# Splitting the Wv products of a fused perceiver block by head

## The chip, the cores and the metric

One core of one Trainium2 chip runs the whole program. The metric is the device time of one execution in microseconds (us), as the median of several runs. PE is TensorE, DVE is VectorE, ACT is ScalarE and POOL is GpSimd.

## What is computed

Three layers are added to `x` (8 batches x 64 queries x 256) one after the other: cross attention to a context of 1601 rows per batch with 16 heads of 64, a linear self attention with 8 heads, and a mixture of 8 experts of which each token takes 2. The change touches the cross attention alone, and in it only the product with the value weights. Cut to that:

```
xn     = layernorm(layernorm(x)) * gamma + beta
scores = (xn @ w_q)_h @ (context @ w_k)_h^T / 8        # per batch and head h
attn   = softmax(scores)
out_h  = attn_h @ (context @ w_v)_h                     # 64 x 64 per batch and head
x      = x + tanh(gate) * (concat(out_h) @ w_out + b_out)
```

The kernel never builds `context @ w_v`. It computes `U_h = attn_h @ context` (64 queries x 256) and then `U_h @ w_v_h` (256 x 64), which is the same by associativity.

## The kernel before, in words

The queries of two heads of one batch (2 x 64) fill 128 columns, and four such pairs make a group of 512 columns: 16 groups (`NG`), two for each batch. Within a group the 1601 context rows are taken in 13 steps of 128 (`SJ`; the last has 65). The kernel is written slot by slot, one slot per context step, 208 slots in all; the steps of one group are spread over later slots, so that the engines overlap. Each engine runs its own list in program order and waits on counting semaphores. 52 slots are written out, then a loop runs 3 times over 52 slots, then comes a drain in which the last group ends while the first 128-token tiles of the following layers (`chain`) begin.

In a slot PE does `scores` (six products of 512 columns in fp32r into the bank pair `sps`) and `times_context` (twelve products of some 256 columns in fp32r into `scp`), in some slots also transposes, and in slot 8 of a group (`V_WV`) `times_wv`, for the group two before. DVE and ACT make the softmax in between: `running_max`, `minus_max`, `exps`, `low_part`.

At the end of a group DVE normalises `U` (`take_u`, L903), PE transposes it in fp32 into `wps` (L1207), ACT copies it to `ut_sb` (L667), and `times_wv` multiplies it: for each of the four head pairs `t` and each half `dt` of the 256 context features one fp32 product. Its stationary operand is `wv_sb` of two heads (128 columns), its moving operand is `ut_sb[:, t, dt, :]`, the 128 query columns of the same two heads. The result is a 128 x 128 block in PSUM of which only the two 64 x 64 blocks on the diagonal mean something (head 0 with head 0's queries, head 1 with head 1's). The fp32 product appears in the trace as two pairs of a weight load (LDWEIGHTS) and a MATMUL, so a visit to `times_wv` is 8 products and 16 such pairs, and there are 16 visits. Then, in slot 9 (`V_O`), DVE's `take_o` copies the two diagonal blocks of all four pairs into `oT` with two instructions of 64 partitions x 256 (L911 and L912), and bank 0 of `wps` is free for the next `transpose_max`. `head_rows` is `(slice(0, 64), slice(64, 128))`, `Q` is 64, `P` is 128, `GT` is 4, `DT` is 2.

Other products of this kernel that have a part in what follows: L1334 (fp32, 128 weight columns, 64 moving columns), L1284 (fp32, 128 weight columns, 256 moving columns), L1424 (an fp32 transpose with 8 weight columns and 128 moving columns), L1431 (fp32, on 8 of the 128 rows, 128 weight columns, 256 moving columns), and L1367 (fp32r, 512 moving columns).

Of the kernel before, what the change touches and what calls it, by code (L numbers as in the profile page):

```python
# [34 lines left out]
P = 128  # L35
B, Q, D = 8, 64, 256
# [4 lines left out]
DT = D // P  # L41
TPB = H * Q // P
GT = 4
# [64 lines left out]
def linear(i, f):  # L108

    if isinstance(i, int):  # L110
        return f(i)
    return i * (f(2) - f(1)) + f(1)


def build(nc, x, ctx_n, ctx_t, gamma, beta, w_q, w_kt, w_v, w_out, b_out, gate, Wq, Wk, Wv, Wo, bo,
          W_router, b_router, W1, b1, W2, b2, out):
    with ExitStack() as es:
        def sb(name, shape, dt=F32):
            return es.enter_context(nc.sbuf_tensor(name, shape, dt))

        def sem(name):
            return es.enter_context(nc.semaphore(name))
# [97 lines left out]
        ut_sb = sb("ut_sb", [P, GT, DT, P])  # L220
# [45 lines left out]
        wps = es.enter_context(nc.psum_tensor("wps", [P, 2, 512], F32))  # L266
# [50 lines left out]
        o_ok = sem("o_ok")  # L317
# [23 lines left out]
        head_rows = (slice(0, Q), slice(Q, P))  # L341
# [32 lines left out]
        def small_h(f):  # L374

            return slice((f % (FT // 2)) * P, (f % (FT // 2) + 1) * P)
# [10 lines left out]
        def hbank(f):  # L387
            return [trp[0], trp[1], up, wp][f % 4]
# [404 lines left out]
        def _(dve):  # L793
# [11 lines left out]
            for r in range(2):  # L805
# [14 lines left out]
                for m in range(MT):  # L820
                    ins = dve.tensor_scalar(xn[:, m, :], src[:, m, :], mv[:, m, 0:1], rstd[:, m:m + 1],
                                            ALU.subtract, ALU.mult)
# [14 lines left out]
            for t in range(TPB):  # L837
# [4 lines left out]
                if t < 4:  # L842
                    ts_ = slice(t * TPB // 4, (t + 1) * TPB // 4)
# [61 lines left out]
            def take_o(i, u, tok):  # L905

                half = u // SJ % GPB
                ts_ = slice(half * GT, (half + 1) * GT)
                v = wps[:, 0, :].rearrange("p (t q) -> p t q", t=GT)
                dve.wait_ge(wv_ok, linear(i, lambda q: q * (PASS // SJ) + u // SJ - 1))  # L910
                dve.tensor_copy(oT[0:Q, ts_, tok], v[0:Q, :, 0:Q])  # L911
                dve.tensor_copy(oT[Q:P, ts_, tok], v[Q:P, :, Q:P]).then_inc(o_ok, 1)  # L912

            def slot(i, u, k):
                if L_SUB <= k < NSLOT + L_SUB:
                    minus_max(i, u - L_SUB)
                if L_LO <= k < NSLOT + L_LO:
                    low_part(i, u - L_LO)
                if 1 <= k <= NSLOT:
                    running_max(i, u - 1)  # L920
                if u % SJ == V_MR and SJ <= k < NSLOT + SJ:
                    column_max(i, u)
                if u % SJ == V_U and k >= 2 * SJ:
                    take_u(i, u)
                if u % SJ == V_O and k >= 2 * SJ:
                    b = u // (2 * SJ) - 1
                    if isinstance(i, int):
                        take_o(i, u, slice((i * 2 + b) * Q, (i * 2 + b + 1) * Q))
                    else:
                        take_o(i, u, bass.ds(i * (2 * Q) + (b + 2) * Q, Q))  # L930
# [194 lines left out]
        def _(pe):  # L1125

            pe.wait_ge(ident_ok, 1)
            for m in range(MT):
                pe.wait_ge(xn_ok, m + 1)
                for dt in range(DT):  # L1130
                    ins = pe.transpose(trp[dt][:, m * P:(m + 1) * P], xn[:, m, dt * P:(dt + 1) * P], ident[:])
# [4 lines left out]
            for t in range(TPB):  # L1136
                if t >= GT:
                    pe.wait_ge(pro_ql, t - GT + 1)
                for dt in range(DT):
                    if t == 0:  # L1140
                        pe.wait_ge(pro_trc, dt + 1)
                    ins = pe.matmul(scp[:, t % GT, :], wq_sb[:, dt, t * P:(t + 1) * P], xnT[:, dt, :],
                                    start=dt == 0, stop=dt == DT - 1)
# [4 lines left out]
            for t in range(TPB):  # L1148
                for dt in range(DT):
# [5 lines left out]
                    for c, (w, v) in enumerate(((wkt_hi, qT_hi), (wkt_hi, qT_lo), (wkt_lo, qT_hi))):  # L1155
                        for par in range(2):
                            ins = pe.matmul(scp[:, 2 * dt + par, :], w[:, par, t, dt * P:(dt + 1) * P], v[:, t, :],
                                            start=c == 0, stop=c == 2)
# [52 lines left out]
            def times_wv(i, u):  # L1211
                half = u // SJ % GPB
                if isinstance(i, int) and u == 2 * SJ + V_WV:
                    pe.wait_ge(tw_in, 16 * NTW)
                pe.wait_ge(utc_ok, linear(i, lambda q: (q * (PASS // SJ) + u // SJ - 1) * 2))
                for t in range(GT):
                    h0 = (half * GT + t) * P
                    for dt in range(DT):
                        ins = pe.matmul(wps[:, 0, t * P:(t + 1) * P], wv_sb[:, dt, h0:h0 + P], ut_sb[:, t, dt, :],  # L1219
                                        start=dt == 0, stop=dt == DT - 1)  # L1220
                ins.then_inc(wv_ok, 1)

            def transpose_max(i, u):
# [18 lines left out]
            def slot(i, u, k):  # L1242
                if k < NSLOT:
                    scores(i, u)
                if u % SJ == V_MT and SJ <= k < NSLOT + SJ:
                    transpose_max(i, u)
                if u % SJ == V_MB and SJ <= k < NSLOT + SJ:
                    spread_max(i, u)
                if L_PV <= k < NSLOT + L_PV:
                    times_context(i, u - L_PV)  # L1250
                if u % SJ == V_UT and k >= 2 * SJ:
                    transpose_u(i, u)
                if u % SJ == V_WV and k >= 2 * SJ:
                    times_wv(i, u)
# [154 lines left out]
            for f in range(FT):  # L1409
                c, n = h_cols(1), 0  # L1410
                for dt in range(DT):
                    for w, v in ((w1_hi, lnT_hi), (w1_hi, lnT_lo), (w1_lo, lnT_hi)):
                        ins = pe.matmul(hbank(f // (FT // 2))[:, small_h(f)], w[:, 0, dt, f * P:(f + 1) * P],
                                        v[:, dt, c], start=n == 0, stop=n == 5)
# [8 lines left out]
            for m in range(MT):  # L1423
                ins = pe.transpose(hbank(3)[0:NE, m * P:(m + 1) * P], gw[:, m, :], ident[:])  # L1424
# [5 lines left out]
            for m in range(MT):  # L1430
                ins = pe.matmul(hbank(2 + m // 2)[:, m % 2 * D:(m % 2 + 1) * D], gwT[:, m * P:(m + 1) * P], b2_sb[:],  # L1431
                                start=True, stop=True)
# [15 lines left out]
            for m in range(MT):  # L1448
                pe.wait_ge(yc_ok, (NE - 1) * MT + m - (MT - 1))
                ms = slice(m * P, (m + 1) * P)  # L1450
                for f in range(FT):
                    if m == 0:
                        pe.wait_ge(hl_ok, NE * FT + f + 1)
                    pe.matmul(scp[:, m, :], h_hi[:, f, ms], w2_sp[:, 1, f, :], start=f == 0, stop=False)
                    ins = pe.matmul(scp[:, m, 0:D], h_lo[:, f, ms], w2_sp[:, 1, f, 0:D],
                                    start=False, stop=f == FT - 1)
# [54 lines left out]
```

## Time and profile before

| | |
|---|---|
| median of 3 runs | 1005.5 us (1004.74 to 1005.71) |
| the profiled execution's own time | 1003.76 us |
| its span, first to last instruction | 1002.0 us |
| mean granted TensorE clock | 0.993 |
| PE busy (matmul) / PE weight loads | 952.7 us / 824.8 us |
| DVE busy / ACT busy / POOL busy | 751.1 / 503.6 / 571.3 us |

A record of a MATMUL lasts longer than the distance to the next one, because matmuls are pipelined; what a product costs is therefore read from start to start. Rows of the timeline merge equal neighbours: start, length of the whole run, and how many. Times in the timeline count from the start of the span.

### The profile page before, as it was taken

Reading aid. Unit: us, or ns where it says so; the run is one execution under the profiler, and the core shown is the slowest. Engines: PE = TensorE matmul, PEld = TensorE weight load, DVE = VectorE, ACT = ScalarE, POOL = GpSimd, SP = SyncE. Lnnn points to the kernel's source line nnn. Section 1 sums busy time; section 2 is a strip of 40 time slices with the busy share of each in tenths; the row PEclk is TensorE's granted clock in tenths of the full one; section 3 lists DMA queues with packets and bytes.
Section 4 is the critical chain, followed back from the end, with each engine's and each line's share of the span. In section 5 each row is a group of like instructions: output and inputs, shape, how many; then the busy total and the mean of one; then the engine's idle time right before and its main releaser. Section 6 shows DMA issues by size and latency. Waiting matters only on the chain.

```text
span 1002.0 us, 17582 instructions
## 1 busy us (share of the span) xinstructions
PE 952.7 (95%) x5732; PEld 824.8 (82%) x5732; DVE 751.1 (75%) x1181; ACT 503.6 (50%) x853; POOL 571.3 (57%) x609
## 2 busy tenths in 40 slices
PE   5899999999999999999999999999998699999998
PEld 2567988998889888899888888888886588888887
DVE  7647777977978868787787887876776676888776
ACT  3336655656565655556556565664452342433432
POOL 5767668948957866894895786730000342454440
PEclk9999999999999999999999999999999889999999
DMA  5584112211211221121221121101004022222200
GB/s 163 189 288 119 51 38 56 67 38 52 69 41 57 64 53 42 57 62 37 56 72 36 55 65 51 43 14 63 1 1 168 1 84 85 84 85 84 84 1 22
DMA packets 76182, 67.55 MB, mean 67 GB/s; under 512 B 7984, under 2 KB 72768, under 8 KB 76096
## 3 DMA queue, kind: packets, MB, share of 16 engines
q1 hardware_dynamic: 76096, 66.41, 22.2%
q8 instruction: 52, 0.85, 0.4%
q14 instruction: 34, 0.28, 0.1%
HBM read 58.01 MB, written 8.39 MB: 66 GB/s over the span
## 4 chain that ended last, share of the span: by engine, by line
PE 81%; DVE 12%; issue 2%; ACT 2%; DMA 2%; POOL 0%; SPq 0%; DVEq 0%; POOLq 0%
PE sps L1178 27%; PE scp L1193 9%; PE scp L1195 9%; PE scp L1194 9%; PE scp L1381 5%; PE sps L1367 5%; PE wps L1367 4%; PE wps L1219 3%; PE scp L1382 2%; DVE u_sb L903 2%; DMA qk_scratch<-oT 1%; DVE st L868 1%; DVE pt_lo L893 1%; PE sps L1284 1%; PE sps L1304 1%
## 5 line engine op out<-in xcount | busy, mean ns | idle before, releaser
L1193 PE MATMUL scp<-cn,pt_hi 128*128 128x258 f32 (+1 forms) x832 | 239.8, 288 | 3.6 <-DVE pt_lo L893 2.8
L1195 PE MATMUL scp<-cn,pt_lo 128*128 128x258 f32 (+1 forms) x832 | 234.9, 282 | 0.0
L1194 PE MATMUL scp<-cn,pt_hi 128*128 128x256 f32 (+1 forms) x832 | 234.9, 282 | 0.0
L650 ACT ACTIVATE st<-sps 128x512 f32<-128x512 f32 (+1 forms) x208 | 123.6, 594 | 159.2 <-PE sps L1178 158.3
L893 DVE TENSOR_TENSOR pt_lo<-st,pt_hi 128x512 fp32r<-128x512 f32 (+1 forms) x208 | 192.7, 926 | 7.2 <-ACT pt_hi L659 7.2
L868 DVE TENSOR_TENSOR st<-st,mbc 128x512 f32<-128x512 f32 (+1 forms) x208 | 156.6, 753 | 44.6 <-ACT mbc L673 37.3
L1178 PE MATMUL sps<-qk_hi,ct_hi 128*128 128x512 f32 (+1 forms) x416 | 167.8, 403 | 12.9 <-ACT st L650 5.6
L656 ACT ACTIVATE st<-st 128x512 f32<-128x512 f32 (+1 forms) x208 | 130.3, 626 | 93.9 <-DVE st L868 93.3
L1193 PEld LDWEIGHTS scp<-cn,pt_hi 128*128 128x128 f32 (+1 forms) x832 | 156.9, 189 | 13.7 <-DVE pt_lo L893 5.7
L1178 PE MATMUL sps<-qk_hi,ct_lo 128*128 128x512 f32 (+1 forms) x416 | 164.3, 395 | 0.0
L1194 PEld LDWEIGHTS scp<-cn,pt_hi 128*128 128x128 f32 (+1 forms) x832 | 157.3, 189 | 7.5 <-issue 0.2
L1178 PE MATMUL sps<-qk_lo,ct_hi 128*128 128x512 f32 (+1 forms) x416 | 163.4, 393 | 0.0
L558 POOL TENSOR_TENSOR cn<-raw,zero 128x256 fp32r<-128x256 f32 (+1 forms) x104 | 81.7, 786 | 133.8 <-PE scp L1195 122.6
L1195 PEld LDWEIGHTS scp<-cn,pt_lo 128*128 128x128 f32 (+1 forms) x832 | 157.8, 190 | 0.0
L879 DVE TENSOR_TENSOR cmax<-cmax,sps 128x512 f32<-128x512 f32 x192 | 130.7, 681 | 34.1 <-ACT st L650 33.5
L659 ACT ACTIVATE pt_hi<-st 128x512 fp32r<-128x512 f32 (+1 forms) x208 | 131.5, 632 | 7.6
L560 POOL TENSOR_TENSOR cn<-raw,cn 128x256 fp32r<-128x256 f32 (+1 forms) x104 | 99.1, 953 | 8.2
L1178 PEld LDWEIGHTS sps<-qk_hi,ct_hi 128*128 128x128 f32 (+1 forms) x416 | 76.6, 184 | 31.3 <-issue 11.9
L560 POOL TENSOR_TENSOR ct_lo<-raw,ct_hi 128x256 fp32r<-128x256 f32 (+1 forms) x104 | 95.7, 920 | 8.2
L558 POOL TENSOR_TENSOR ct_hi<-raw,zero 128x256 fp32r<-128x256 f32 (+1 forms) x104 | 93.5, 899 | 9.6 <-DMA raw<-ctx_t 9.6
L1178 PEld LDWEIGHTS sps<-qk_hi,ct_lo 128*128 128x128 f32 (+1 forms) x416 | 76.4, 184 | 20.2
L1178 PEld LDWEIGHTS sps<-qk_lo,ct_hi 128*128 128x128 f32 (+1 forms) x416 | 76.7, 184 | 10.4
(210 smaller groups left out, 1523.1 us busy)
## 6 DMA issues: line engine op xcount, KB each, us to landing
w_raw<-W SPq DMA_DIRECT2D x16, 1024.0 KB, 7.4
raw<-ctx_t SPq DMA_DIRECT2D x96, 128.0 KB, 2.2
raw<-ctx_n SPq DMA_DIRECT2D x96, 128.0 KB, 2.0
raw<-qk_scratch SPq DMA_DIRECT2D x60, 128.0 KB, 2.1
qk_scratch<-oT SPq DMA_DIRECT2D x4, 1024.0 KB, 6.1
qk_scratch<-oT SPq DMA_DIRECT2D x4, 896.0 KB, 4.2
wq_sb<-w_q SPq DMA_DIRECT2D x1, 1024.0 KB, 4.9
wkt_sb<-w_kt SPq DMA_DIRECT2D x1, 1024.0 KB, 7.8
```

Source lines behind the costliest of these rows:

```text
L558: pool.tensor_tensor(hi, src, z.broadcast_to(tuple(src.shape)), ALU.add).then_inc(split_hi, 1)
L560: pool.tensor_tensor(lo, src, hi.bitcast(F32), ALU.subtract).then_inc(done, 1)
L650: act.activation(st[0:rows(j), par, j, :], sps[0:rows(j), u % 2, :], ACT.Copy).then_inc(out_ok, 1)
L656: act.activation(p, p, ACT.Exp).then_inc(exp_ok, 1)
L659: act.activation(pt_hi[0:rows(j), r, :], p, ACT.Copy).then_inc(hi_ok, 1)
L868: dve.tensor_tensor(p, p, mbc[0:rows(j), par, :], ALU.subtract).then_inc(sub_ok, 1)
L879: dve.tensor_tensor(m, m, src, ALU.max).then_inc(max_ok, 1)
L893: dve.tensor_tensor(pt_lo[0:rows(j), r, :], st[0:rows(j), par, j, :], pt_hi[0:rows(j), r, :].bitcast(F32), ALU.subtract).then_inc(lo_ok, 1)
L1178: ins = pe.matmul(sps[0:rows(j), u % 2, :], a[:, dt, cols], v[:, par, dt, :], start=c == 0, stop=c == 5)
L1193: pe.matmul(scp[:, t, 0:D + 2], hi, cn[0:rows(j), j, 0:D + 2], start=j == 0, stop=False)
L1194: pe.matmul(scp[:, t, 0:D], hi, cn[0:rows(j), j, D + 2:CNW], start=False, stop=False)
L1195: ins = pe.matmul(scp[:, t, 0:D + 2], lo, cn[0:rows(j), j, 0:D + 2], start=False, stop=j == SJ - 1)
```

## The change

`times_wv` issues two products where it had one: for each head of the pair one with that head's 64 weight columns and that head's 64 moving columns, into 64 of the output partitions (0 to 63 for the first head, 64 to 127 for the second) and 64 columns of the bank. A visit then has 16 products in place of 8, and the two heads alternate. The results of the four pairs lie side by side in 256 columns, and `take_o` copies them with one instruction of 128 partitions x 256. Semaphores, slots and all other work stay.

```
@@ take_o
-                v = wps[:, 0, :].rearrange("p (t q) -> p t q", t=GT)
                 dve.wait_ge(wv_ok, linear(i, lambda q: q * (PASS // SJ) + u // SJ - 1))
-                dve.tensor_copy(oT[0:Q, ts_, tok], v[0:Q, :, 0:Q])
-                dve.tensor_copy(oT[Q:P, ts_, tok], v[Q:P, :, Q:P]).then_inc(o_ok, 1)
+                dve.tensor_copy(oT[:, ts_, tok],
+                                wps[:, 0, 0:GT * Q].rearrange("p (t q) -> p t q", t=GT)).then_inc(o_ok, 1)
@@ times_wv
                     for dt in range(DT):
-                        ins = pe.matmul(wps[:, 0, t * P:(t + 1) * P], wv_sb[:, dt, h0:h0 + P], ut_sb[:, t, dt, :],
-                                        start=dt == 0, stop=dt == DT - 1)
+                        for hr in head_rows:
+                            ins = pe.matmul(wps[hr, 0, t * Q:(t + 1) * Q],
+                                            wv_sb[:, dt, h0 + hr.start:h0 + hr.stop], ut_sb[:, t, dt, hr],
+                                            start=dt == 0, stop=dt == DT - 1)
```

## Rows read from the trace of the kernel before

**Rows 1.** The page: busy us of PE, and granted clock in 40 slices.
```profile
PE 952.7 (95%) x5732; PEld 824.8 (82%) x5732; DVE 751.1 (75%) x1181; ACT 503.6 (50%) x853; POOL 571.3 (57%) x609
PEclk9999999999999999999999999999999889999999
```

**Rows 2.** The page: the chain that ended last, shares of the span by line.
```profile
PE sps L1178 27%; PE scp L1193 9%; PE scp L1195 9%; PE scp L1194 9%; PE scp L1381 5%; PE sps L1367 5%; PE wps L1367 4%; PE wps L1219 3%; PE scp L1382 2%; DVE u_sb L903 2%; DMA qk_scratch<-oT 1%; DVE st L868 1%; DVE pt_lo L893 1%; PE sps L1284 1%; PE sps L1304 1%
```

**Rows 3.** The chain in order of time, 255 to 310 us: start, us, what.
```profile
261.34 1.78 PE wps L1219 x16
263.13 1.40 PE sps L1178 x6
```

**Rows 4.** All instructions on the tile wps: durations in ns min/median/max.
```profile
L1219 PEld LDWEIGHTS wps<-ut_sb,wv_sb x256: 187/192/192, 137.6 to 772.1; 128*128 128x128 f32 x128
...
L911 DVE COPY oT<-wps x16: 408/417/417, 139.7 to 772.9; 64x256 f32 x12, 64x256 f32<-64x256 f32 x4
L912 DVE COPY oT<-wps x16: 427/429/430, 140.1 to 773.3; 64x256 f32 x12, 64x256 f32<-64x256 f32 x4
```

**Rows 5.** Timeline of PE around one visit: start us, us, line, operation, tiles.
```profile
261.18 1.95 PE L1219 MATMUL wps<-ut_sb,wv_sb 128*128 128x128 f32 x16
262.88 0.48 PE L1178 MATMUL sps<-qk_hi,ct_hi 128*128 128x512 f32 x1
263.20 0.39 PE L1178 MATMUL sps<-qk_lo,ct_hi 128*128 128x512 f32 x1
```

**Rows 6.** Timeline of PE, 16 pairs with 64 moving columns.
```profile
733.16 1.95 PE L1334 MATMUL sps<-ke,cbd 128*128 128x64 f32 x16
734.94 0.61 PE L1311 MATMUL sps<-ident,ke 128*128 128x128 f32 x4
```

**Rows 7.** Timeline of PE, 16 pairs with 256 moving columns.
```profile
690.21 3.61 PE L1284 MATMUL sps<-wout_sb,oT 128*128 128x256 f32 x16
693.66 0.60 PE L1229 MATMUL wps<-ident,cmax 128*128 128x128 f32 x4
```

**Rows 8.** Weight loads of 65 columns (L1178, last context step), ns min/median/max.
```profile
L1178 PEld LDWEIGHTS sps<-qk_hi,ct_hi x2: 134/134/135, 230.0 to 230.6; 128*65 128x65 f32 x2
```

**Rows 9.** Timeline of PE around the products on 8 rows.
```profile
841.08 0.40 PE L1367 MATMUL sps<-lnT_lo,w_hi 128*128 128x512 f32 x1
841.31 0.39 PE L1367 MATMUL sps<-lnT_hi,w_lo 128*128 128x512 f32 x1
841.63 1.99 PE L1431 MATMUL wps<-b_sb,gwT 8*128 8x256 f32 x8
843.55 0.50 PE L1367 MATMUL sps<-lnT_hi,w_hi 128*128 128x512 f32 x1
843.89 0.39 PE L1367 MATMUL sps<-lnT_lo,w_hi 128*128 128x512 f32 x1
```

**Rows 10.** Timeline of PE around the transposes with 8 weight columns.
```profile
839.59 0.28 PE L1382 MATMUL scp<-w_sp,h_lo 128*128 128x256 f32 x1
839.70 0.60 PE L1424 MATMUL wps<-ident,gw 128*8 128x128 f32 x4
```

**Rows 11.** Timeline of DVE after one visit.
```profile
221.92 0.42 DVE L911 COPY oT<-wps 64x256 f32 x1 [1.53 <-PE wps L1219]
222.34 0.43 DVE L912 COPY oT<-wps 64x256 f32 x1
...
224.13 0.69 DVE L879 TENSOR_TENSOR cmax<-cmax,sps 128x512 f32<-128x512 f32 x1
```

**Rows 12.** Timeline of PE, the scores that wait for that maximum.
```profile
227.27 0.40 PE L1178 MATMUL sps<-qk_hi,ct_hi 128*128 128x512 f32 x1
```

**Rows 13.** Timeline of all engines after the last visit.
```profile
773.32 0.43 DVE L912 COPY oT<-wps 64x256 f32<-64x256 f32 x1
773.63 0.66 PE L1317 MATMUL sps<-ident,qe 128*128 128x128 f32 x4 [0.69 <-ACT kn L715]
774.12 3.62 PE L1284 MATMUL scp<-wout_sb,oT 128*128 128x256 f32 x16
```

## The prediction

> **What bounds the kernel.** I read the page first. PE is busy for 952.7 of 1002 us and its clock is granted almost throughout [rows 1]; a busy PE is not yet PE at its peak, so the next view is the chain of waits. It is made of PE's lines, with the changed line L1219 holding 3% of the span and no DVE line above 2% [rows 2]. In order of time, the reader should see the visit to L1219 stand in that chain with its whole length, 1.78 us, and the scores of the next slot follow at once [rows 3]. So whatever a visit gains or loses on PE goes one to one into the time, 16 times. 1% of the span is about 35% of what all visits cost (16 x 1.78 = 28.5 us), and that is the frame: a visit that vanished would be worth 2.8%.
>
> **What a visit costs now.** From its first MATMUL to the first of the scores are 1.70 us, and the next one comes after 0.32 us where 0.23 is usual in that row's stream (841.08 to 841.31); 1.70 + 0.09 = 1.79 us for 16 pairs of weight load and MATMUL, 111 ns a pair [rows 5, 9]. Two things could set these 111 ns. L1334 has half the moving columns (64) and the same 128 weight columns, and its 16 pairs take 1.78 us, 111 ns a pair: fewer moving columns alone buy nothing [rows 6]. L1284 has 256 moving columns and takes 3.45 / 16 = 216 ns a pair, 0.84 ns per moving column [rows 7]; 128 columns would be 108 ns. So now both sides, 128 weight columns and 128 moving columns, stand at the same height. The change halves both.
>
> **The new products.** A visit has 32 pairs with 64 weight and 64 moving columns. No row has such a pair. From the moving side: 64 x 0.84 = 54 ns. From the weight side: a load of 65 columns lasts 134 ns where one of 128 lasts 192 (L1219) [rows 4, 8]; that is some 0.9 ns a column, so 64 fewer take about 55 ns off the 111 and leave 56 to 57. The slower side sets the pace: 57 ns, and 32 x 57 = 1.82 us. The bounds are 54 ns a pair from [rows 7], and 111 ns if a pair has a floor of its own that [rows 6] can't be told from; faster than 54 only if the two heads overlap (a rival below). I take 57, because in [rows 7] a pair's time follows its columns with hardly a constant. Against 1.79 us this is +0.03 to +0.04 us a visit: half as many useless multiplications, but twice as many pairs at half the length, and the balance is zero.
>
> **Entering and leaving a part of the array.** The old products use all rows and all columns, as do all products around them; the new ones write 64 of the 128 output partitions. The trace has a block that uses part of the array, L1431 on 8 of 128 rows. The MATMUL before it is followed after 0.32 us instead of 0.23 (+0.09); its 8 pairs with 256 moving columns take 1.92 us where 8 x 0.216 = 1.73 (+0.19); and the first fp32r product after it takes 0.34 instead of 0.23 (+0.11). Together 0.39 us for going in and out, in which no weight load hides behind the MATMUL before [rows 7, 9]. In going in, a load of 64 columns is 0.055 us shorter than one of 128, so I take 0.33 us a visit; bounds 0 and 0.39. The nearest row against it is L1424: 8 weight columns, and it follows after the usual 0.11 us [rows 10], but it is a transpose and writes from partition 0, so nothing forces it into a part of the array, while the second head's output at partition 64 does. The Trainium skill (TensorEngine Tiling (Array Packing), Key Properties) says that a change of the tiling mode, not merely of the tile, drains TensorE. By that the columns pay as the rows do in [rows 9], and alternating between the two halves within a visit pays nothing; without the rule the cost of part columns would be as open as its two bounds, and the sum by it is the same +0.33.
>
> **DVE.** Two copies of 0.42 and 0.43 us become one of 128 x 256, which by their durations takes 0.43 us: 0.42 us less a visit [rows 4, 11]. It is hidden: DVE had idled 1.53 us for the visit, and the next thing that PE wants from behind the copies, the maximum that ends at 224.82, is wanted by the scores at 227.27, 2.4 us later [rows 11, 12]. Behind the last visit the copies end at 773.75, and the product that reads them starts only at 774.12, when L1317 has left PE [rows 13]. So 0; if the cover were gone the saving would be 16 x 0.42 = 6.7 us. A longer visit delays DVE and the softmax behind it by 0.37 us, well inside the same 2.4.
>
> **Sum.** 0.04 + 0.33 = 0.37 us a visit, 16 x 0.37 = 5.9 us. The profiled execution would go from 1003.76 to 1009.7 us; the median of the runs is 1.7 us above it, so 1005.5 + 5.9 = 1011.4 us. The likeliest case's own range is 1008 to 1014. About 0.2% (2 us) is what a measurement of this kernel can tell from no change.
>
> **Rival 1, faster: the halves overlap.** The two heads use different columns of the array and alternate, so each pair could run beside its neighbour. Then 16 double pairs at 57 ns are 0.91 us, with the 0.33 us of going in and out 1.24 against 1.79: -0.55 us a visit, 996.7 us; without the switch cost -0.88 us, 991.4 us. It decides from where the 32 pairs take under 1.79 - 0.33 = 1.46 us, 46 ns a pair. For it speaks that they share no output and no weights; against it that all weight loads in the trace follow each other at one load's length, in [rows 6] even where the moving side is half idle, so that the load path, which stays full (32 x 64 columns), would hold 57 ns. The trace has no pair of neighbours on different columns. The Trainium skill (same page and section) states that different tiles can load weights and multiply in parallel, with up to twice the speed at 64 columns; that is this rival, its time would be the 996.7 us, and no row here shows it. Chance 0.22.
>
> **Rival 2, no change: no switch cost for columns.** As in [rows 10], the loads go on hiding. Then 0.04 x 16 = 0.6 us: 1006.1 us. Chance 0.15.
>
> **Rival 3, much slower: a pair has a floor, or its load isn't hidden.** At 111 ns a pair, 32 take 3.55 us: +1.76, with the switch +2.09 us a visit, 1039 us. At 80 ns, half way, 2.56 us: +1.10, 1023 us. For it: no pair in the rows is shorter than 108 to 111 ns whichever side is small. The Trainium skill (TensorE: Matmul & The Clock Gate, Part 3) says that a weight load overlaps a MATMUL in flight only when it goes to other rows of the array; then load and MATMUL would add to some 111 ns, the 1039 us. The trace does not agree for full columns: 16 loads and 16 MATMULs of 108 ns and more each fit in 1.79 us [rows 5]. Chance 0.18, two thirds of it near 1023.
>
> **Numbers.** My forecast, serial pairs at their columns' length plus the switch, has 0.45, since the balance of zero rests on two rows and the switch on one that measures rows and not columns. Faster 0.24 (rival 1, and a little of DVE's saving surfacing), same 0.13, slower 0.63. The range of 8 in 10 leaves out the fast end of rival 1 and the slow end of rival 3: 996 to 1026 us.
>
> **What would show it.** A visit, from its first MATMUL to the scores, of about 32 x 57 = 1.8 us plus delays at both ends, with the first weight load no longer beside the MATMUL before it: right. A distance of 57 ns between MATMULs shows the pace, 28 shows overlap, 111 the floor. One copy of 0.43 us on DVE with idle time before it, and no new wait of PE for DVE. The prediction is wrong if the visit is shorter than 1.7 us, if the switch is missing, or if PE's clock or a loop's start moves the time by more than the visits do.

## The result, and the profile after

The changed kernel takes 995.19 us (median; 994.19 to 996.96, 4 runs) where the one before takes 1005.37 us: ratio 0.9901, 95% interval 0.9884 to 0.9919. Measured a second time, 996.25 us against 1005.02, ratio 0.9912 (0.9895 to 0.9928). The two profiled executions are 8.1 us apart: 995.64 us against 1003.76. It is faster by about 0.9%, where 0.6% slower was forecast. The case that occurred is rival 1.

The page of the changed kernel, busy time and granted clock (against [rows 1]):

```profile
PE 945.0 (95%) x5988; PEld 814.4 (82%) x5988; DVE 747.2 (75%) x1165; ACT 503.2 (51%) x853; POOL 570.7 (57%) x609
PEclk9999999999999999999999999999999799999999
```

PE has 256 MATMUL records more and is busy 7.7 us less. The clock is nearly as before, 0.991 on average against 0.993. In the chain in order of time (start, us, what) a visit still stands with its whole length, now 1.08 us where [rows 3] has 1.78:

```profile
259.40 1.08 PE wps L1219 x32
260.48 1.59 PE sps L1177 x6
```

The timeline of PE around one visit of the changed kernel, against [rows 5]:

```profile
218.26 0.28 PE L1194 MATMUL scp<-cn,pt_lo 128*128 128x258 f32 x1
218.47 1.15 PE L1219 MATMUL wps<-ut_sb,wv_sb 128*64 128x64 f32 x32
219.55 0.50 PE L1177 MATMUL sps<-qk_hi,ct_hi 128*128 128x512 f32 x1
219.90 0.39 PE L1177 MATMUL sps<-qk_lo,ct_hi 128*128 128x512 f32 x1
```

All 32 pairs of weight load and MATMUL fit in 219.55 - 218.47 = 1.08 us. Before them there are now 0.21 us to the last MATMUL of L1194 where 0.12 is usual (+0.09), and behind them the second product of the scores comes after 0.35 us where 0.23 is usual (+0.11). A visit costs 0.09 + 1.08 + 0.11 = 1.28 us. Before it cost 1.79. The weight loads of the same stretch show the way in and out: the first of the visit and the first of the scores start with their own MATMUL, not 0.11 us ahead of it.

```profile
218.47 1.01 PEld L1219 LDWEIGHTS wps<-ut_sb,wv_sb 128*64 128x64 f32 x32
219.55 0.19 PEld L1177 LDWEIGHTS sps<-qk_hi,ct_hi 128*128 128x128 f32 x1
```

How the 32 pairs lie can be read by counting the MATMULs of L1219 in ever longer windows from the visit's start. The columns are window, its length, PE busy with the count in brackets, granted clock, DMA share and GB/s:

```profile
218.46:218.50 0.04, 0.03 (x2) 1.00 0.76 256
218.46:218.57 0.11, 0.10 (x2) 1.00 0.53 177
218.46:218.60 0.14, 0.13 (x4) 1.00 0.53 176
218.46:218.63 0.17, 0.16 (x4) 1.00 0.47 157
218.46:218.66 0.20, 0.19 (x6) 1.00 0.43 144
```

They start two at a time, one of each head, and the next two follow after some 58 ns. That is the 57 ns I had expected of one pair, with two pairs in it. Only the first step is longer, since its weight load is not hidden. Sixteen steps of 58 ns are 0.93 us, so 0.15 of the 1.08 us belong to going in and out, as do the 0.09 and 0.11 beside the block: 0.35 us in all.

The period of two groups, from a visit to the second one after it, shows what it is worth. Before, from 261.18 [rows 5] to

```profile
343.39 1.95 PE L1219 MATMUL wps<-ut_sb,wv_sb 128*128 128x128 f32 x16
```

are 82.21 us. In the changed kernel

```profile
259.32 1.15 PE L1219 MATMUL wps<-ut_sb,wv_sb 128*64 128x64 f32 x32
...
340.43 1.15 PE L1219 MATMUL wps<-ut_sb,wv_sb 128*64 128x64 f32 x32
```

are 81.11 us: -1.10 us for two visits, -0.55 each, and -8.8 us for sixteen. Read from the visit alone it was -0.51; where the other 0.04 us come from was not settled. DVE's timeline behind a visit (against [rows 11]) has one copy of 128 partitions, and DVE still idles for the visit, 0.81 us, and again later:

```profile
219.80 0.42 DVE L910 COPY oT<-wps 128x256 f32 x1 [0.81 <-PE wps L1219]
...
221.88 0.69 DVE L879 TENSOR_TENSOR cmax<-cmax,sps 128x512 f32<-128x512 f32 x1 [0.46 <-ACT st L650]
```

### The profile page after: what moved, and what is told of

The parts are those of the page before. It is cut to its first block, busy times and chain, and to the rows that moved or that the text cites. A ratio compares the mean times of both kernels' runs of the same rounds, so it can differ in the third digit from the quotient of the medians.

```text
span 993.8 us, 18066 instructions
## 1 busy us (share of the span) xinstructions
PE 945.0 (95%) x5988; PEld 814.4 (82%) x5988; DVE 747.2 (75%) x1165; ACT 503.2 (51%) x853; POOL 570.7 (57%) x609
## 4 chain that ended last, share of the span: by engine, by line
PE 82%; DVE 11%; issue 2%; ACT 2%; DMA 1%; POOL 1%; SPq 0%; DVEq 0%; POOLq 0%
PE sps L1177 27%; PE scp L1192 9%; PE scp L1194 9%; PE scp L1193 9%; PE scp L1382 5%; PE sps L1368 4%; PE wps L1368 4%; PE scp L1383 2%; DVE u_sb L903 2%; PE wps L1219 2%; DVE st L868 1%; PE scp L1156 1%; PE sps L1285 1%; PE sps L1305 1%; DMA qk_scratch<-oT 1%
## 5 line engine op out<-in xcount | busy, mean ns | idle before, releaser
L1194 PE MATMUL scp<-cn,pt_lo 128*128 128x258 f32 (+1 forms) x832 | 234.8, 282 | 0.0
L868 DVE TENSOR_TENSOR st<-st,mbc 128x512 f32<-128x512 f32 (+1 forms) x208 | 158.8, 763 | 43.3 <-ACT mbc L673 37.8
L1194 PEld LDWEIGHTS scp<-cn,pt_lo 128*128 128x128 f32 (+1 forms) x832 | 157.7, 190 | 0.0
L560 POOL TENSOR_TENSOR ct_lo<-raw,ct_hi 128x256 fp32r<-128x256 f32 (+1 forms) x104 | 90.8, 873 | 8.2
```

The costliest lines, as they stand in the source:

```text
L560: pool.tensor_tensor(lo, src, hi.bitcast(F32), ALU.subtract).then_inc(done, 1)
L868: dve.tensor_tensor(p, p, mbc[0:rows(j), par, :], ALU.subtract).then_inc(sub_ok, 1)
L1194: ins = pe.matmul(scp[:, t, 0:D + 2], lo, cn[0:rows(j), j, 0:D + 2], start=False, stop=j == SJ - 1)
```

## The experiments

The theory after the result (A): the two halves of the columns work side by side, so what counts is the longer half's list at 58 ns a pair, plus some 0.35 us for going in and out. It has two rivals: that a pair of this small size simply takes 34 ns, whatever its neighbour (B), and that the gain is DVE's single copy (C). Where nothing else is said, a kernel is the changed one with the edit shown.

**Same products, the heads in turn.**

```
-                for t in range(GT):
-                    for dt in range(DT):
-                        for hr in head_rows:
+                for hr in head_rows:
+                    for t in range(GT):
+                        for dt in range(DT):
                             ins = pe.matmul(wps[hr, 0, t * Q:(t + 1) * Q], ...
```

> The changed kernel with the same 16 products per visit in another order: all eight of the first head, then all eight of the second, so that neighbours use the same half of the columns. Theory A (the halves run side by side, a step of 58 ns holds one pair of each half, and going in and out costs about 0.35 us): 31 steps of 58 ns = 1.80 us + 0.35 = 2.15 us a visit against 1.79 before, +0.36 us x 16 = +5.8 us, so about 1011 us. Theory B (a pair of this size simply takes 34 ns, whatever its neighbour): as the changed kernel, 995 us. Theory C (the gain is DVE's single copy, PE's order is indifferent): 995 us too.

Measured 1006.94 us (10 runs), ratio to before 1.0017 (1.0007 to 1.0026). The whole gain is gone with nothing changed but the order. Its timeline of PE:

```profile
261.95 0.28 PE L1194 MATMUL scp<-cn,pt_lo 128*128 128x258 f32 x1
262.15 1.90 PE L1219 MATMUL wps<-ut_sb,wv_sb 128*64 128x64 f32 x32
263.98 0.50 PE L1177 MATMUL sps<-qk_hi,ct_hi 128*128 128x512 f32 x1
264.32 0.39 PE L1177 MATMUL sps<-qk_lo,ct_hi 128*128 128x512 f32 x1
...
344.74 1.90 PE L1219 MATMUL wps<-ut_sb,wv_sb 128*64 128x64 f32 x32
```

The block is 1.83 us against 1.08. That it is so close to the 1.82 us of my forecast for 32 serial pairs is partly chance: 0.15 us of it are for going in and out, as in the 1.08, and the pairs alone take 29 steps of 58 ns, 1.68 us. Counting MATMULs in growing windows finds them one by one:

```profile
220.56:220.60 0.04, 0.03 (x1) 1.00 0.72 231
220.56:220.67 0.11, 0.10 (x1) 1.00 0.51 159
220.56:220.70 0.14, 0.13 (x2) 1.00 0.41 125
220.56:220.75 0.19, 0.18 (x3) 1.00 0.30 92
```

B and C are refuted. A was too high by 0.12 us a visit: with the same ends as the changed kernel the block is 0.75 us longer, 13 steps of 58 ns, so it has 29 steps and not the 31 that were expected: about three pairs at the joint of the two runs did overlap. The time rose by 1.8 us, not by 5.8. From visit to visit (262.15 to 344.74) the period of two groups is 82.59 us, +0.19 us a visit, or +3.0 us. The rest is for the most part in another place, at the turns of the loop (below).

**Runs of four on one half.** The two inner loops of the changed kernel exchanged:

```
-                    for dt in range(DT):
-                        for hr in head_rows:
+                    for hr in head_rows:
+                        for dt in range(DT):
```

> The changed kernel with the order of the two inner loops exchanged: per head pair both products of the first head, then both of the second, so four weight-and-MATMUL pairs in a row use the same half. Theory A with issue in program order (only the last pair of a run lies beside the first of the next run): 8 runs of 4, 25 steps of 58 ns = 1.45 us + 0.35 = 1.80 us a visit, as before the change: about 1005.5 us. Theory A with a reach of several pairs ahead: 16 steps as in the changed kernel, 995 us. Theories B and C: 995 us.

996.56 us, ratio 0.991 (0.989 to 0.993), as the changed kernel. Its visit:

```profile
218.12 1.20 PE L1219 MATMUL wps<-ut_sb,wv_sb 128*64 128x64 f32 x32
219.25 0.50 PE L1177 MATMUL sps<-qk_hi,ct_hi 128*128 128x512 f32 x1
```

1.13 us, 0.05 more than alternating. So a pair need not be the neighbour of its partner: from four pairs back the other half still gets its work in time, from sixteen back it does not. Issue strictly beside the neighbour, the variant of A that gave 1005.5 us, is refuted.

**One head alone.** `for hr in head_rows` becomes `for hr in head_rows[0:1]`. The kernel leaves out the second head's products, so it does not compute the layer any more and serves only to time the first head's.

> The changed kernel without the second head's products (they are left out; the second head's rows hold no result). Theory A: the second head ran beside the first and cost nothing, so 16 pairs take 16 steps of 58 ns and the visit stays at 1.28 us: about 995 us. Theory B: 16 pairs of 34 ns are half the block, -0.5 us a visit, about 987 us.

996.5 us, ratio 0.9909 (0.989 to 0.9928). The visit of 16 pairs:

```profile
218.92 1.15 PE L1219 MATMUL wps<-ut_sb,wv_sb 128*64 128x64 f32 x16
220.00 0.50 PE L1177 MATMUL sps<-qk_hi,ct_hi 128*128 128x512 f32 x1
```

Half of the products take 1.08 us as well. The second head is free, to within the 0.01 us that the view resolves. B, by which 16 pairs are half a block, is refuted here too.

**Two copies.** `take_o` with one copy for each 64 partitions, as before.

> The changed kernel with its single copy of 128 partitions x 256 cut into two of 64 partitions x 256, as before the change. Theory A (all of the gain is PE's, DVE's copy is hidden): as the changed kernel, 995 us, within 1 us. Theory C (the gain is DVE's): up to +0.42 us x 16 = +6.7 us, 1002 us.

995.96 us, ratio 0.9911 (0.9894 to 0.9927), beside 0.9912 for the changed kernel on the same chip. DVE has its two copies again:

```profile
220.55 0.42 DVE L911 COPY oT<-wps 64x256 f32 x1 [0.81 <-PE wps L1220]
220.99 0.43 DVE L912 COPY oT<-wps 64x256 f32 x1
```

The kernel is no slower for them, so the copy saved is hidden, as the prediction had it. C is refuted a second time.

**The changed kernel again**, on that chip:

> The changed kernel again, with more rounds. Counted from the visits: -0.51 us x 16 = -8.1 us, ratio 0.992. If something beside the visits gives another 2 us, as the medians of the first measurement had it: ratio 0.990.

996.25 us, ratio 0.9912 (0.9895 to 0.9928): -8.8 us. The first measurement had -10.2 us, with an interval of -8.1 to -11.7 that holds this value. That 16 times the -0.55 us of the period give the same -8.8 is partly chance. From the first visit to the last the two profiles of the changed kernel are 9.1 to 9.4 us shorter than the two of before (623.8 and 623.9 us against 632.9 and 633.2), in part since the turns of the loop cost less as well (below). Behind the last visit the two profiles of before differ by 2.0 us among themselves (231.4 and 233.5), and those of the changed kernel, 232.6 and 232.4, lie between them.

**A full product in the middle.**

```
                 for t in range(GT):
+                    if t == GT // 2:
+                        pe.matmul(wps[:, 0, 3 * P:4 * P], wv_sb[:, 0, 0:P], ut_sb[:, t, 0, :], start=True, stop=True)
```

> The changed kernel with one product of 128 weight columns and 128 moving columns more in the middle of each visit, written to columns of the bank that nothing reads. If going in and out of the half columns costs 0.35 us each time: 0.22 us for its two pairs + 0.35 us for a second way in and out = +0.57 us x 16 = +9.1 us, about 1004.5 us. If the switch is paid only once per visit or not at all: +0.22 us x 16 = +3.5 us, about 998.7 us.

1004.28 us (10 runs), ratio 0.9993 (0.9983 to 1.0003). The visit:

```profile
220.41 0.69 PE L1221 MATMUL wps<-ut_sb,wv_sb 128*64 128x64 f32 x16
221.02 0.49 PE L1217 MATMUL wps<-ut_sb,wv_sb 128*128 128x128 f32 x2
221.44 0.69 PE L1221 MATMUL wps<-ut_sb,wv_sb 128*64 128x64 f32 x16
222.05 0.50 PE L1177 MATMUL sps<-qk_hi,ct_hi 128*128 128x512 f32 x1
```

One product of two pairs, worth 0.22 us in the full array, makes the block 1.64 us long, +0.56. The other 0.34 us are a second way in and out. In time, the ratio lies 0.008 to 0.009 above those of the changed kernel, 8 to 9 us, where 16 x 0.56 = 9.0 would be expected. With its ends (0.61 + 0.09 + 0.11) half a visit costs 0.81 us, where eight full pairs at 111 ns cost 0.89: at this length the switch has eaten nearly the whole gain.

**Merged visits.** If the switch is what is left, half of the visits should go. ACT keeps both groups of a batch in a doubled `ut_sb`, and one visit multiplies all eight head pairs; the waits count in twos. `GPB` is the 2 groups of a batch, `TPB` its 8 head pairs.

```
-        ut_sb = sb("ut_sb", [P, GT, DT, P])
+        ut_sb = sb("ut_sb", [P, GPB, GT, DT, P])
...
-                for t in range(GT):
-                    h0 = (half * GT + t) * P
+                if u // SJ % GPB == 0:
+                    return
+                for t in range(TPB):
+                    h0 = t * P
...
-                ins.then_inc(wv_ok, 1)
+                ins.then_inc(wv_ok, 2)
...
-                dve.tensor_copy(oT[:, ts_, tok],
-                                wps[:, 0, 0:GT * Q].rearrange("p (t q) -> p t q", t=GT)).then_inc(o_ok, 1)
+                dve.tensor_copy(oT[:, :, tok],
+                                wps[:, 0, :].rearrange("p (t q) -> p t q", t=TPB)).then_inc(o_ok, 2)
```

The room in SBUF comes from `mrow` and `xn`, which now share places with tensors of other stages (`gwT` and the second half of `ut_sb`).

> The changed kernel with the visits of a batch's two groups made as one: ACT keeps both groups' transposed U in a doubled ut_sb, PE multiplies all eight head pairs in one visit (32 products, 512 columns of the bank), DVE copies them with one instruction of 128 x 512. If going in and out costs 0.35 us each time, eight of the sixteen fall away: -2.8 us against the changed kernel, about 992.4 us. If the switch isn't paid for on the path: no change, 995 us. If the later copy or the doubled wait delays a follower: slower than 995 us.

992.69 us, ratio 0.9877 (0.9861 to 0.9894); a second time 992.15 us, 0.9867 (0.9852 to 0.9882). Its visit:

```profile
338.75 2.08 PE L1221 MATMUL wps<-ut_sb,wv_sb 128*64 128x64 f32 x64
340.77 0.50 PE L1178 MATMUL sps<-qk_hi,ct_hi 128*128 128x512 f32 x1
341.11 0.39 PE L1178 MATMUL sps<-qk_lo,ct_hi 128*128 128x512 f32 x1
```

64 pairs take 2.02 us, with the ends 2.22 in place of 2 x 1.28: -0.34 us for each switch saved, -2.7 us for eight. Measured are -3.6 us beside the changed kernel on the same chip, a little more than the switches account for.

**The same cut on another product.** The repeat of merged visits was to give its own time on the same chip:

> The kernel with merged visits again, beside the one with the cbd products cut as well, so that the two can be compared on one chip: 992.7 us by its first measurement.

Beside it ran merged visits with the cbd products of the linear attention (L1334 before) cut in the same way; here both halves stream the same moving columns.

```
-                            ins = pe.matmul(bank[:, t * P + b * Q:t * P + (b + 1) * Q], cbd[:, r, b, t, :],
-                                            lqT[:, r, t, b * Q:(b + 1) * Q], start=True, stop=True)
+                            for hr in head_rows:
+                                ins = pe.matmul(bank[hr, t * P + b * Q:t * P + (b + 1) * Q], cbd[:, r, b, t, hr],
+                                                lqT[:, r, t, b * Q:(b + 1) * Q], start=True, stop=True)
```

> The kernel with merged visits, and in addition the products with cbd in the linear attention (L1334 before, 16 pairs per 128-token tile, four tiles, 128 weight columns and 64 moving columns) cut into two halves of 64 weight columns that write to the two halves of the output partitions. If the halves run side by side here too: 16 steps of 58 ns + 0.35 us = 1.28 us in place of 1.78 us, -0.5 us for each of four tiles, all of it on the path in that stretch: -2 us against merged visits alone, about 990.7 us. If the stretch is bound by DVE and ACT: no change, 992.7 us. If the halves don't overlap on a moving operand that both share: +0.4 us a tile, 994 us.

987.52 us, ratio 0.9829 (0.9816 to 0.9843), the fastest kernel of this study: -17 us against before, -4.6 against its neighbour with merged visits alone. The block of one tile without the cut, and then with it:

```profile
719.56 1.89 PE L1337 MATMUL sps<-ke,cbd 128*128 128x64 f32 x16
721.29 0.50 PE L1314 MATMUL sps<-ident,ke 128*128 128x128 f32 x3
```

```profile
719.71 1.15 PE L1338 MATMUL sps<-ke,cbd 128*64 128x64 f32 x32
720.79 0.55 PE L1314 MATMUL sps<-ident,ke 128*128 128x128 f32 x3
```

It is more than the 2 us expected. One part of the difference is that one of the four tiles runs at half clock (granted clock 0.56 and 0.50 in the two blocks, mostly or wholly the level of 1.2 GHz), where the block falls from 3.2 to 1.9 us:

```profile
768.93 3.39 PE L1337 MATMUL sps<-ke,cbd 128*128 128x64 f32 x16 [0.42 <-DVE cbd L1009]
772.11 1.17 PE L1301 MATMUL scp<-lnT,lw_sb 128*128 128x128 f32 x4
```

```profile
767.84 1.97 PE L1338 MATMUL sps<-ke,cbd 128*64 128x64 f32 x32 [0.41 <-DVE cbd L1009]
769.74 1.45 PE L1301 MATMUL scp<-lnT,lw_sb 128*128 128x128 f32 x6
```

The other part is that less of the stretch from 760 to 810 us was spent at half clock, some 10 us against 17, mean granted clock 0.90 against 0.83. In both kernels the clock fell behind a stretch in which PE had partly idled (busy for 1.01 of the 2 us from 766 on without the cut, for 0.58 of the 2 us from 764 on with it). Runs of equal mean clock tell how much the cut is worth without this part: at 0.991 it took 988.9 us against 992.1 to 992.5, at 0.993 988.3 against 990.6, so 2.3 to 3.6 us. The other three runs with the cut had 0.995 and took 986.9 to 987.5 us; no run without it had that clock. Whether the cut itself brings the better clock stays open.

**Quarters.** The cut of the changed kernel, carried on to weights of 32 columns at output partitions 0, 32, 64 and 96.

```
-                        for hr in head_rows:
-                            ins = pe.matmul(wps[hr, 0, t * Q:(t + 1) * Q],
-                                            wv_sb[:, dt, h0 + hr.start:h0 + hr.stop], ut_sb[:, t, dt, hr],
+                        for x in range(0, P, P // 4):
+                            hr = head_rows[x // Q]
+                            ins = pe.matmul(wps[x:x + P // 4, 0, t * Q:(t + 1) * Q],
+                                            wv_sb[:, dt, h0 + x:h0 + x + P // 4], ut_sb[:, t, dt, hr],
                                             start=dt == 0, stop=dt == DT - 1)
```

> The changed kernel with each product's 64 weight columns cut again into two of 32: a visit has 64 pairs in four quarters of the columns. If four run side by side, a step stays at the 54 to 58 ns that 64 moving columns need: 16 steps, as the changed kernel, 996 us. If a step has room for two pairs only: 32 steps, 1.86 + 0.35 us a visit, +0.93 us x 16 = +15 us, 1011 us. If each weight-and-MATMUL pair costs an issue time above 14 ns, four of them outgrow the step: between the two, by that issue time.

994.72 us, ratio 0.9903 (0.9888 to 0.9918): twice the pairs in the same time.

```profile
259.43 1.10 PE L1220 MATMUL wps<-ut_sb,wv_sb 128*32 128x64 f32 x64
260.46 0.50 PE L1177 MATMUL sps<-qk_hi,ct_hi 128*128 128x512 f32 x1
```

64 pairs in 1.03 us are 16 ns a pair. Four run side by side, and a step is still some 58 ns though each of its weight loads has half the columns. This speaks for the 64 moving columns, as in [rows 7], and against the length of a load as what sets the step. It does not prove it: a limit of some 14 ns for issuing each pair would give the same number with quarters, and no run tells the two apart. The finer cut brings nothing that the halves had not brought.

**The turns of the loop.** The visits of the kernel with the heads in turn account for +3.0 us, and it was 1.8 us slower. The rest was looked for in a second profile of this kernel and of the one before.

> The kernel before, profiled a second time. In its first profile the period of two groups that holds the first turn of the loop is 43.7 us where its neighbours of the kind are 41.4 (2.3 us more); in the changed kernel it is 42.2 against 40.9 (1.3 more). If the 1.0 us between them belongs to the kernels, the second profile shows 2.3 again; if it is the chance of one execution, it shows something near 1.3.

> The kernel with the two heads in turn, profiled a second time, for the same question: its first profile has 42.9 against 41.6 at the first turn of the loop and 42.7 against 41.6 at the second (1.3 and 1.1 more). If that is its own, it is 0.8 to 1.0 us faster at each turn than before, which would explain why its time rose by 1.8 us where its visits account for 3.3; if chance, the second profile shows other values and its time about 1008 us.

The first visit behind the loop's first turn, before and with the heads in turn; the visits ahead of it, at 343.39 and 344.74, stand above:

```profile
386.41 1.95 PE L1219 MATMUL wps<-ut_sb,wv_sb 128*128 128x128 f32 x16
```

```profile
386.97 1.90 PE L1219 MATMUL wps<-ut_sb,wv_sb 128*64 128x64 f32 x32
```

The distance from visit to visit alternates between 40.8 and 41.4 us before (41.0 and 41.6 with the heads in turn), and a turn falls into the shorter one. Before, it is 43.02 us here, where 40.80 are usual: the turn costs 2.2 us (1.9 in the second profile). With the heads in turn it is 42.23 where 41.01 are usual, 1.2 us (1.6 in the second profile). Both turns of the loop together cost 4.1 and 4.4 us before in the two profiles, and 2.2 and 2.5 us with the heads in turn. So it is a property of the kernel, and not of one execution, that its turns cost 1.5 to 2.2 us less. With +3.0 us from the visits this leaves +0.8 to +1.5, and the measured +1.8 has an interval of +0.7 to +2.6. In the changed kernel both turns cost 3.4 and 3.3 us, 0.7 to 1.1 less than before. The idle time of PE at the turn shows a part of it:

```profile
358.25 0.47 PE L1178 MATMUL sps<-qk_hi,ct_hi 128*128 128x512 f32 x1 [1.58 <-issue]
```

```profile
359.18 0.47 PE L1177 MATMUL sps<-qk_hi,ct_hi 128*128 128x512 f32 x1 [1.05 <-POOL qk_lo L560]
```

At both turns together PE idles for 1.58 + 1.48 = 3.06 us before the change and 1.42 + 1.71 = 3.13 in the second profile, and with the heads in turn for 1.05 + 0.86 = 1.91 and 1.40 + 0.79 = 2.19. Why the turns differ was not settled. They move by more than a microsecond between kernels that differ in nothing near them: with runs of four both together cost 5.1 us (one profile).

## Why the prediction was wrong

**What bounds the kernel: right.** PE's visits stand on the path whole. What a visit loses comes back in the time: 0.51 to 0.55 us a visit are 8.2 to 8.8 us, and 8.8 and 10.2 us were measured. The clock moved little, but the turns of the loop gave some 0.7 to 1.1 us of their own, which the forecast put at nothing.

**The new products: this step failed.** "32 x 57 = 1.82 us" took the pairs as serial. Issued head after head, a pair does take 58 ns. But two pairs on different halves of the columns share one step, so the alternating block has 16 steps and not 32: 0.93 us, or 1.08 with its share of the switch. The number of steps was twice too high, and this term should have been -0.86 us a visit against 1.79 where it had +0.03 to +0.04. The price of a step, 57 ns, came out right with some luck: "64 fewer take about 55 ns off" does not follow from 0.9 ns a column, which makes 58 and leaves 53, so the moving side's 54 ns would have set the pace. Which of the two sides sets the 58 ns is not shown; the quarters speak for the moving side. The error is small beside the other: 54 ns for each of 32 serial pairs would still have forecast a slower kernel.

**Where the argument against overlap broke.** I held against rival 1 that loads follow each other at one load's length, so that the load path would stay full at 32 x 64 columns. The rows behind that ([rows 6]) show loads into all 128 columns only, and say nothing of loads into different halves. In the changed kernel the loads overlap like the MATMULs do. The Trainium skill (TensorEngine Tiling (Array Packing), Key Properties) says that different tiles can load weights and multiply in parallel, and the trace agrees: 32 loads in 1.01 us. Its sentence was the only evidence on neighbours in different columns, and should have outweighed an extension from other rows; with it rival 1 deserved more than 0.22.

**Entering and leaving: right.** 0.33 us was forecast and 0.34 to 0.35 measured: 1.28 us a visit is 16 x 58 ns + 0.35, a second way in and out costs 0.34, and each saved one gives 0.34 back. A block on a part of the rows ([rows 9]) did price one on a part of the columns.

**DVE: right.** The copy is hidden; two copies take the same time as one.

**The sum.** Rival 1 had its own sum of -0.55 us a visit and 996.7 us, from the same two prices. Measured are 995.2 and 996.3 us. So the rows carried nearly the right number, under the wrong heading. The stated range began at 996 us, just above the first measurement and just below the second.

**Rivals 2 and 3** are out: the switch costs, and a pair has no floor of 80 or 111 ns. Nor is the load of a pair exposed: the rule of the Trainium skill (TensorE: Matmul & The Clock Gate, Part 3) that a load overlaps a MATMUL in flight only on other rows of the array would make the heads in turn take 111 ns a pair, and there they take 58.

## What to carry to other kernels

Where a product wastes half of its output because two independent parts share one stationary operand, cut it by columns of the weights and let the parts alternate: the two halves of the array ran side by side here, also with a moving operand in common, and a step with two equal pieces cost what one piece costs alone (pieces of unequal length were not tried). The order of issue matters: the same products gained nothing when all sixteen pairs of one part came before the other part's, and nearly everything in runs of four. Each block of this kind pays about 0.35 us for leaving and re-entering the full array, so it must be long (16 pairs of 111 ns were, and merging two blocks paid again).

## What was not expected of the hardware

- Two pairs on different halves start at once and share a step of 58 ns; with quarters 64 pairs took 1.03 us, 16 ns a pair.
- The partner need not be the neighbour: with runs of four on one half the block was 1.13 us against 1.08. With runs of sixteen it was 1.83, in which some three pairs overlapped at the joint.
- The price of using a part of the array was nearly the same for 8 of 128 rows (0.39 us with full weight loads) and for 64 of 128 columns (0.34 to 0.35 us with half ones).
